# The whole ring of gathered rows filled one stage earlier, and the table of slots' experts made on partitions

## The chip, the cores and the metric

One core of one Trainium2 chip runs the whole program. The metric is the device time of one execution in microseconds (us). The kernel before takes 2877.39 us, the median of 3 runs (2876.5 to 2879.93).

## The reference, cut to what matters

A graph layer over 6250 nodes and 200000 edges (sorted by destination), then a mixture of 16 experts of which each node uses 2. Both add to the node's row.

```python
w_full = jnp.einsum('rb,bdo->rdo', w_comp, weight)          # R=16 relations from B=8 bases
x_rel = jnp.einsum('nd,rdo->rno', feat, w_full)             # feat = layernorm(x), 256 columns
msg = x_rel[etypes, src] * norm
agg = jax.ops.segment_sum(msg, dst, num_segments=N)
x = x + jax.nn.relu(agg + h_bias + feat @ loop_weight)
...
gate_logits = x @ gate_w + gate_b                           # x here: layernorm of the row
topk_vals, topk_idx = jax.lax.top_k(gate_logits, K)         # K=2 of E=16
topk_w = jax.nn.softmax(topk_vals, axis=-1)
h = jax.nn.relu(jnp.einsum('bsh,ehf->bsef', x, w1) + b1)
expert_out = jnp.einsum('bsef,efh->bseh', h, w2) + b2
...
y = x + moe
return (y - mu) / jnp.sqrt(var + EPS) * gamma + beta
```

## The kernel before, in words

The edges lie in 1568 blocks of 128. A step is one block against one window of 16 destination nodes; a block that crosses into a new window has a step for each, so that there are 1960 steps, seven to a turn. Destinations are dense at low node numbers, so the first window alone fills many blocks, and for these step number and block number are the same.

The stages follow one another as blocks of the program (`edges_in`, `sort_edges`, `steps`, `expand`, `graph_layer`, `route`, `experts`, `combine`). Between two stages all engines meet in a barrier: each engine drains, and none starts the next stage before the last has come. In the profile a barrier stands under the line of the stage that ends: L613 ends `expand` (its `with ctx:`), L891 ends `graph_layer`, L1467 ends `experts`.

**expand** (L607) makes the coefficients of the edges. GpSimd (POOL) fetches 16 groups of edge data by indirect DMA (L684), and between them gathers feature rows of the first blocks into the ring `rows` (L676): one indirect DMA per block, 128 rows of 256 floats. Before, 42 of the ring's 56 slots are filled here. TensorE (PE) and VectorE (DVE) make coefficients of the same groups; the later part goes to DRAM through SyncE's queue (L717), and SyncE waits at the end for these stores (L725).

```python
for q in range(EG + 1):                       # L672
    e.tensor_copy(idx[:, q * GB:(q + 1) * GB], srcT[:, q * GB:(q + 1) * GB]).then_inc(s_list, 1)
...
for j in range(3 * (SG - GR), EG * GB):       # L689
    ahead(j)
```

**graph_layer** (L885) goes through all steps. POOL gathers the remaining blocks in lists of GB = 14 (L978), each list into 14 slots of the ring; the list's indices are copied first (L960). For a list that goes into a slot used before, POOL waits until PE has done the steps of the blocks that lie there:

```python
for q in range(0 if later(i) else EG, IB):    # L965
    if later(i) or q >= RB // GB:
        e.wait_ge(s_P, free[q])               # L968
        e.sem_inc(s_turn, 1)
```

For the first such list, q = 4 (blocks 56 to 69, over blocks 0 to 13), `free[4]` is the first step of block 14, that is 14 steps. SyncE counts the gathered blocks on to PE (L941). PE first clears its accumulators with eight products of zeros (L1083, L1084), then for each turn loads a row of control words (L1166), branches over the code of a finished tile (L1168), waits for rows and coefficients, and issues seven steps, of two matmul records each (L1178). After every 16 windows it multiplies the tile by the bases (L1143). DVE builds the selection matrix of each turn (L1057) three turns ahead at most; for its turn n it waits until PE has done turn n - 4, except that turns 0 to 3 wait for nothing. So DVE's turn 5 starts when PE has done 14 steps. At the start of the stage SyncE and ScalarE also load the stage's weights and features (L934 to L937, L1191, L1195).

**route** (L1268) chooses the experts and sorts the pairs of node and expert into 114 slots of 128 rows. DVE makes the counts by prefix sums; `u` holds for each expert the number of the slot where it ends, the same on every partition. Then for 100 tiles DVE makes two one-hot operands (L1441, L1445) and PE sums their products (L1355). At the end DVE makes the table `slot_x` of the slots' experts (L1447 to L1450), clears `at_rows` (L1451), waits for PE and forms the rows' addresses (L1454 to L1459). Everything on DVE is one chain: each instruction waits for the one before.

Of the kernel before, what the change touches and what calls it, by code (L numbers as in the profile page):

```python
# [5 lines left out]
F32 = mybir.dt.float32  # L6
# [3 lines left out]
AX = mybir.AxisListType  # L10
P = 128
# [5 lines left out]
X, F, K = 16, 512, 2  # L17
# [61 lines left out]
RB = 56  # L79
GB = 14  # L80
QB = 7
IB = 2 * (RB // GB)
EG = RB // GB - 1
CTL_PART = (84, 72, 64, 60)
assert NBLK % RB == 0 and RB % GB == 0 and RB % QB == 0 and sum(CTL_PART) == TURNS and all(n % NS == 0 for n in CTL_PART)
assert all(t + n <= 8 * i <= TURNS for t, n, i in CHUNK)
# [2 lines left out]
SLOTS = (N * K + X * (P - 1)) // P  # L89
# [517 lines left out]
def expand(nc, d, w_comp, ident, tables, pairs, jcol, wcol, spread, dstS, wgtS, coefS, s_got, s_feat, srcT, idx, rows, s_row):  # L607
# [5 lines left out]
    with ctx:  # L613
# [53 lines left out]
        def _(e):  # L667
# [3 lines left out]
            e.iota(pno[:, :], [[0, 1]], base=-U, channel_multiplier=CN, allow_small_or_imprecise_dtypes=True).then_inc(s_const, 1)  # L671
            for q in range(EG + 1):  # L672
                e.tensor_copy(idx[:, q * GB:(q + 1) * GB], srcT[:, q * GB:(q + 1) * GB]).then_inc(s_list, 1)
# [211 lines left out]
def graph_layer(nc, d, a, ctl, pairs, room, wend, srcT, dstS, coefS, ident, wb, lw, hb, gw, s_w, logit, mean, rstd, idx, rows, s_row):  # L885
# [5 lines left out]
    with ctx:  # L891
# [96 lines left out]
        def _(e):  # L988
# [11 lines left out]

            def nodes(tile1, Q):

# [262 lines left out]
            e.wait_ge(s_st, 32 * (NT2 + 1))  # L1265


def route(nc, gate_b, w1, w2, logits, w1s, w2s, s_win, wgt, slot_x, at_rows):  # L1268


    from contextlib import ExitStack
    ctx = ExitStack()
    with ctx:
        def sb(name, shape, dt=F32):
            return ctx.enter_context(nc.sbuf_tensor(name, shape, dt))

        def sem(name):
            return ctx.enter_context(nc.semaphore(name))

        logit = sb("logit_b", [P, NT, X])  # L1280
# [10 lines left out]
        part = sb("part", [P, 1])  # L1291
# [5 lines left out]
        slots = sb("slots", [P, X])  # L1297
        end = [sb(f"end{k}", [P, X]) for k in range(2)]
        first = sb("first2", [P, X])
        slot_no = sb("slot_no", [1, SLOTS + 4])  # L1300
        ge = sb("ge", [1, SLOTS + 4, X])
        sx = sb("sx", [1, SLOTS + 4])
        pos = sb("pos", [P, NT, K], I32)
        part_i = sb("pos_part", [P, NT, K], I32)
        lo, hi, row = (sb(n, [P, NT, K]) for n in ("pos_lo", "pos_hi", "row_no"))
# [9 lines left out]
        psP = [ctx.enter_context(nc.psum_tensor(f"psP{k}", [P, 512], F32)) for k in range(2)]  # L1315
        psI = ctx.enter_context(nc.psum_tensor("psI", [P, 512], F32))
        s_w, s_c, s_d, s_df, s_e, s_b, s_p = (sem(n) for n in ("gate_b", "const", "dve", "diff", "exp", "both", "prefix"))
        s_lane, s_tile, s_inv = sem("lanes"), sem("tiles"), sem("inverse")
        Q = [(0, 25), (25, NT)]
        flat = "p t e -> p (t e)"  # L1320
        blk = ctx.enter_context(nc.Block())
# [11 lines left out]
        @blk.gpsimd  # L1333
        def _(e):
            e.iota(xno[:, :], [[1, X]], base=-X, channel_multiplier=0, allow_small_or_imprecise_dtypes=True).then_inc(s_c, 1)
            e.iota(lane[:, :], [[1, P]], base=0, channel_multiplier=0, allow_small_or_imprecise_dtypes=True).then_inc(s_c, 1)
            e.iota(part[:, :], [[0, 1]], base=0, channel_multiplier=1, allow_small_or_imprecise_dtypes=True).then_inc(s_c, 1)
            e.iota(slot_no[:, :], [[1, SLOTS + 4]], base=0, channel_multiplier=0, allow_small_or_imprecise_dtypes=True).then_inc(s_c, 1)
            e.iota(row[:, :, :].rearrange("p (t m) k -> p t (m k)", m=2), [[K * GN2, NT2], [1, 2 * K]], base=K, channel_multiplier=2 * K, allow_small_or_imprecise_dtypes=True).then_inc(s_c, 1)
            e.iota(tile_no[:, :], [[1, SLOTS]], base=0, channel_multiplier=0, allow_small_or_imprecise_dtypes=True).then_inc(s_c, 1)  # L1340
            e.iota(spare[:, :], [[P, SLOTS]], base=DUMP, channel_multiplier=1, allow_small_or_imprecise_dtypes=True).then_inc(s_c, 1)

        @blk.tensor
        def _(e):
            e.wait_ge(s_b, 1)
            for q, (t0, t1) in enumerate(Q):
                rhs = both[:, t0:t1, :].rearrange(flat)
                e.matmul(psP[q][:, 0:(t1 - t0) * X], tri[:, :], rhs, start=True, stop=True)
                last = e.matmul(psA[q][:, 0:(t1 - t0) * X], ones[:, :], rhs, start=True, stop=True)
            last.then_inc(s_p, 1)  # L1350
            for j in range(NT * K):
                if j % (GT * K) == 0:
                    e.wait_ge(s_lane, j // (GT * K) + 1)
                e.wait_ge(s_tile, j + 1)
                e.matmul(psI[:, 0:SLOTS], in_lane[j // (GT * K) % 2][:, j % (GT * K), :], in_tile[j % D][:, :], start=(j == 0), stop=(j == NT * K - 1)).then_inc(s_inv, 1)  # L1355
# [7 lines left out]
        def _(e):  # L1363
            ch = Chain(e, s_d)
# [4 lines left out]
            def over_e(a):  # L1369
                return a.unsqueeze(2).to_broadcast([P, NT, X])  # L1370

            e.wait_ge(s_c, 7)
            ch.add(e.memset(ones[:, :], 1.0))
            ch.add(e.tensor_scalar(tri[:, :], lane[:, :], part[:, 0:1], None, ALU.is_gt))
            ch.add(e.tensor_scalar(valid[:, :], part[:, :], float(TAIL), None, ALU.is_lt))
# [29 lines left out]
            a, b, sh = cum[0], cum[1], 1  # L1405
            while sh < NT:
                ch.add(e.tensor_copy(b[:, 0:sh, :], a[:, 0:sh, :]))
                ch(e.tensor_tensor(b[:, sh:NT, :], a[:, sh:NT, :], a[:, 0:NT - sh, :], ALU.add))
                a, b, sh = b, a, 2 * sh
# [5 lines left out]
            u, v, sh = end[0], end[1], 1  # L1415
            while sh < X:
                ch.add(e.tensor_copy(v[:, 0:sh], u[:, 0:sh]))
                ch(e.tensor_tensor(v[:, sh:X], u[:, sh:X], u[:, 0:X - sh], ALU.add))
                u, v, sh = v, u, 2 * sh
# [11 lines left out]
            ch(e.tensor_copy(lo[:, :, :], part_i[:, :, :]))  # L1431
            ch(e.tensor_single_scalar(part_i[:, :, :], pos[:, :, :], 7, ALU.arith_shift_right))
            ch(e.tensor_copy(hi[:, :, :], part_i[:, :, :]))

            for j in range(NT * K):
                t, k = divmod(j, K)
# [6 lines left out]
                if j >= D:  # L1443
                    e.wait_ge(s_inv, j - D + 1)
                e.tensor_scalar(in_tile[j % D][:, :], tile_no[:, :], hi[:, t, k:k + 1], row[:, t, k:k + 1], ALU.is_equal, ALU.mult).then_inc(s_tile, 1)  # L1445

            ch(e.tensor_tensor(ge[:, :, :], slot_no[:, :].unsqueeze(2).to_broadcast([1, SLOTS + 4, X]),  # L1447
                               u[0:1, :].unsqueeze(1).to_broadcast([1, SLOTS + 4, X]), ALU.is_ge))
            ch(e.tensor_reduce(sx[:, :], ge[:, :, :], AX.X, ALU.add))
            ch(e.tensor_scalar(slot_x[:, :], sx[:, :], float(X - 1), None, ALU.min))  # L1450
            ch(e.memset(at_rows[:, :, :], 0))  # L1451

            e.wait_ge(s_inv, NT * K)
# [392 lines left out]
def program(nc, a, out):  # L1846
    from contextlib import ExitStack
    ctx = ExitStack()
    d = Scratch(nc)

    with ctx:
        def sb(name, shape, dt=F32):
            return ctx.enter_context(nc.sbuf_tensor(name, shape, dt))

        def sems(name, n):
            return [ctx.enter_context(nc.semaphore(f"{name}{k}")) for k in range(n)]

        ident = sb("ident", [P, P])
        logit = sb("logit", [P, NT + 2, X])
        mean, rstd = sb("mean", [P, NT]), sb("rstd_h", [P, NT])  # L1860
        sent, got, s_row, s_xin, s_out, s_win = sems("sorted", 2), sems("got", 8), sems("row", RB // QB), sems("x_in", 2), sems("x_out", 2), sems("w_in", 4)
        with nc.sbuf_tensor("ident_i", [P, P], F32) as ident_i:
            identity(nc, ident, ident_i)
        gnn(nc, d, a, ident, sent, got, s_row, logit, mean, rstd)
        clear_semaphores(nc)
        wgt = sb("wgt", [P, NT, K])
        slot_x = sb("slot_x", [1, SLOTS + 4], I32)
        at_rows = sb("at_rows", [P, SLOTS + 4, 2], I32)
        with nc.sbuf_tensor("w1s", [P, X, HC, F], F32) as w1s, nc.sbuf_tensor("w2s", [P, X, FC, H], F32) as w2s:
            route(nc, a["L0_ffn_gate_b"], a["L0_ffn_w1"], a["L0_ffn_w2"], logit, w1s, w2s, s_win, wgt, slot_x, at_rows)  # L1870
            experts(nc, d, a["L0_ffn_b1"], a["L0_ffn_b2"], w1s, w2s, s_win, ident, slot_x, at_rows, s_xin, s_out)
        combine(nc, d, ident, mean, rstd, wgt, a["L0_ffn_gamma"], a["L0_ffn_beta"], out)

# [20 lines left out]
```

## Time and profile before

| | |
|---|---|
| median of 3 runs | 2877.39 us |
| the profiled execution | 2876.8 us |
| its span, first to last instruction | 2875.0 us |
| PE busy (matmul) | 2245.9 us, 78% |
| POOL busy | 1821.4 us, 63% |
| DVE busy | 964.7 us, 34% |
| `expand`, `graph_layer`, `route`, `experts` begin at about | 95, 180, 2191, 2276 us |

Busy time is what the engine's own instructions take; the time that POOL's sequencer needs between two indirect DMAs is not in it and stands as idle "issue". A row of a timeline gives the start, the duration, the engine and line, the operation with the tiles it writes and reads, and in brackets the idle time before it with what ended it. An engine name with a q is its sequencer: waits, branches, drains. All times are from the start of the span.

### The profile page before, as it was taken

To read this page: it belongs to the slowest core of one execution; us is meant where nothing else is said; L and a number is where in the kernel's file an instruction comes from. 1 tells how busy PE (TensorE), PEld (TensorE's weight loads), DVE (VectorE), ACT (ScalarE), POOL (GpSimd) and SP (SyncE) were. 2 spreads that over 40 slices of the span, in tenths; PEclk is the share of its full clock that TensorE was granted. 3 is DMA by queue.
4 is the path that set the end of the run, shared out by engine and by line. 5 is a ranking of instruction groups with operands and counts; after the bars stand their busy time and mean duration, and the time that the engine had idled before them with its cause. 6 is when DMAs were issued, how large, how long until landed. Compare 5 with 4: busy or idle time off the path is not lost. (4 is left out here: it accounts for less than half of the span.)

```text
span 2875.0 us, 41253 instructions
## 1 busy us (share of the span) xinstructions
PE 2245.9 (78%) x11563; PEld 1848.7 (64%) x11564; DVE 964.7 (34%) x2255; ACT 591.0 (21%) x1382; POOL 1821.4 (63%) x2003
## 2 busy tenths in 40 slices
PE   1676566766776787888888998999993699999977
PEld 0455444644665666676676776878782588888765
DVE  6762111121212221222232232242425733333338
ACT  2100000101011111122222222232330022222245
POOL 0467777777777777777777777777710144554444
PEclk9787777887888898999999999999996899999998
DMA  6363333343334434444444444444425211111246
GB/s 234 91 192 104 104 105 105 104 122 115 108 116 122 119 118 116 118 134 120 119 121 131 130 123 127 122 126 127 129 49 189 100 63 64 62 63 61 62 156 241
DMA packets 146352, 338.78 MB, mean 118 GB/s; under 512 B 36707, under 2 KB 56323, under 8 KB 146148
## 3 DMA queue, kind: packets, MB, share of 16 engines
q0 software_dynamic: 89392, 245.59, 29.4%
q1 hardware_dynamic: 39311, 59.54, 6.0%
q10 hardware_dynamic: 17588, 32.88, 3.4%
q8 instruction: 34, 0.56, 0.1%
q14 instruction: 27, 0.21, 0.0%
HBM read 293.10 MB, written 47.97 MB: 119 GB/s over the span
## 5 line engine op out<-in xcount | busy, mean ns | idle before, releaser
L978 POOL DMA_INDIRECT rows<-feat,idx x1526 | 1447.9, 949 | 450.0 <-issue 436.3
L1178 PE MATMUL psW<-rows,S 128*128 x3920 | 1062.6, 434 | 358.0 <-SPq L941 325.4
L1178 PEld LDWEIGHTS psW<-rows,S 128*128 128x128 f32 x3920 | 843.0, 219 | 573.0 <-issue 435.3
L1057 DVE TENSOR_TENSOR S<-psHere,coefS 128x896 f32<-128x896 f32 x280 | 303.2, 1091 | 1385.9 <-PE psW L1178 1379.8
L1236 ACT COPY z<-psW 128x512 f32<-128x512 f32 x196 | 114.9, 586 | 1363.1 <-PE psW L1178 1360.6
L1143 PE MATMUL psG<-wb,zT 128*128 128x256 f32 (+1 forms) x1600 | 353.5, 379 | 0.0
L1143 PEld LDWEIGHTS psG<-wb,zT 128*128 128x128 f32 (+1 forms) x1600 | 300.6, 188 | 44.7
L1509 POOL DMA_INDIRECT xs<-y_rows,at x114 | 116.3, 1020 | 211.3 <-DVE os L1624 211.0
L1565 PE MATMUL psH<-xT,w1x 128*128 128x128 f32 x1840 | 228.0, 277 | 0.3 <-DVE w1x L1607 0.3
L1538 ACT ACTIVATE hT<-psH,b1T 128x128 f32<-128x128 f32 x460 | 131.5, 368 | 428.1 <-PE psH L1565 428.1
L1565 PEld LDWEIGHTS psH<-xT,w1x 128*128 128x128 f32 x1840 | 215.9, 193 | 1.3 <-issue 0.6
L1574 PE MATMUL psO<-w2s,hT 128*128 x912 | 215.7, 379 | 0.0
L1574 PEld LDWEIGHTS psO<-w2s,hT 128*128 128x128 f32 x912 | 164.6, 190 | 17.6
L1522 POOL DMA_INDIRECT expert_rows<-os,at x114 | 120.5, 1057 | 38.5 <-issue 36.3
L1624 DVE TENSOR_TENSOR os<-psO,b_b 128x256 f32<-128x256 f32 x114 | 48.4, 425 | 238.2 <-PE psO L1574 238.2
L1130 PE MATMUL psZ<-ident,z 128*128 128x128 f32 x784 | 113.7, 283 | 13.6 <-ACT zT L1250 8.9
L1238 ACT COPY psW<-zero 128x512 f32<-128x512 f32 x196 | 115.5, 589 | 6.2
L1250 ACT COPY zT<-psZ 128x512 f32<-128x512 f32 x196 | 108.0, 589 | 18.6 <-PE psZ L1130 18.6
L1130 PEld LDWEIGHTS psZ<-ident,z 128*128 128x128 f32 x784 | 83.7, 141 | 36.2 <-ACT zT L1250 20.3
L1555 PE MATMUL psX<-ident,xs 128*128 128x128 f32 x232 | 49.4, 295 | 43.4 <-DMA xs<-y_rows,at 37.6
L1607 DVE COPY w1x<-w1s 128x1024 f32 x116 | 80.0, 690 | 0.2 <-issue 0.2
L1555 PEld LDWEIGHTS psX<-ident,xs 128*128 128x128 f32 x232 | 25.3, 142 | 78.5 <-issue 54.6
(256 smaller groups left out, 1429.8 us busy)
## 6 DMA issues: line engine op xcount, KB each, us to landing
rows<-feat,idx POOLq DMA_INDIRECT x1568
g<-expert_rows SPq DMA_DIRECT2D x24, 512.0 KB, 6.1
w1s<-in_L_ffn_w SPq DMA_DIRECT2D x8, 1024.0 KB, 10.9
w2s<-in_L_ffn_w SPq DMA_DIRECT2D x16, 512.0 KB, 10.9
feat<-rows SPq DMA_DIRECT2D x24, 256.0 KB, 4.4
fts<-feat ACTq DMA_DIRECT2D x24, 256.0 KB
h<-in_x ACTq DMA_DIRECT2D x24, 256.0 KB
y_rows<-y ACTq DMA_DIRECT2D x24, 256.0 KB
```

Of the source, the lines that this page charges most:

```text
L978: e.indirect_dma_start(rows[:, at * H:(at + 1) * H], None, d.feat, bass.IndirectOffsetOnAxis(ap=idx[:, q * GB + u:q * GB + u + 1], axis=0) ...
L1057: e.tensor_tensor(S[h0 + h][:, :].rearrange("p (s b n) -> p s b n", s=U, b=B), both[:, h * U:(h + 1) * U, :].unsqueeze(2).to_broadcast([P, ...
L1130: last = e.transpose(to[:, k * P:(k + 1) * P], z[:, w * H + c * P:w * H + (c + 1) * P], ident[:, :])
L1143: last = e.matmul(psG[0:Q, m * H:(m + 1) * H], zT[:, at:at + Q], wb[:, c, b, :], start=False, stop=(c == HC - 1 and b == B - 1))
L1178: e.matmul(psW[:, bass.ds(bank[u], H)], S[h][:, u * ZC:(u + 1) * ZC], rows[:, bass.ds(slot[u], H)], start=False, stop=True, skip_group_che ...
L1236: e.copy(z[:, 2 * k * H:2 * (k + 1) * H], bank).then_inc(s_z, 1)
L1238: e.copy(bank.rearrange("p (w o) -> p w o", w=2), zero[:, :].unsqueeze(1).to_broadcast([P, 2, H])).then_inc(s_clear, 1)
L1509: e.indirect_dma_start(xs[k][:, :], None, d.y, bass.IndirectOffsetOnAxis(ap=column, axis=0)).then_inc(s_in[k], 16)
L1522: e.indirect_dma_start(d.two, bass.IndirectOffsetOnAxis(ap=at[k][:, 1:2], axis=0), os_[k][:, :], None).then_inc(s_out[k], 16)
L1538: last = e.activation(hT[k][:, c * P:(c + 1) * P], psH[k][:, c * P:(c + 1) * P], ACT.Relu, bias=b1T[:, bass.ds(ex * FC + c, 1)])
L1565: last = e.matmul(psH[k][:, f * P:(f + 1) * P], w1x[k][:, c * F + f * P:c * F + (f + 1) * P], xT[k][:, c * P:(c + 1) * P], start=(c == 0), ...
L1574: last = e.matmul(psO[k][:, 0:H], hT[k][:, c * P:(c + 1) * P], w2s[:, bass.ds(ex, 1), c, :].rearrange("p e f -> p (e f)"), start=(c == 0), ...
```

## The change

Two edits that have nothing to do with one another.

The first is one constant: EG, the number of lists of 14 gathered in `expand`, goes from 3 to 4. All 56 slots of the ring are gathered there; five lists of indices are copied instead of four; and `graph_layer` starts its loop at q = 4, the first list that waits.

The second is in `route`. Slot numbers no longer lie along one partition but across partitions: each partition p compares the 16 ends with its own number, sums and clips (three small instructions, before the 100 tiles). PE turns this column into a row with the identity matrix, ahead of the tiles' products, and DVE copies the row out of PSUM to `slot_x` after the tiles. The iota of slot numbers goes.

```diff
-EG = RB // GB - 1
+EG = RB // GB
...
-def route(nc, gate_b, w1, w2, logits, w1s, w2s, s_win, wgt, slot_x, at_rows):
+def route(nc, ident, gate_b, w1, w2, logits, w1s, w2s, s_win, wgt, slot_x, at_rows):
...
-        slot_no = sb("slot_no", [1, SLOTS + 4])
-        ge = sb("ge", [1, SLOTS + 4, X])
-        sx = sb("sx", [1, SLOTS + 4])
+        ge = sb("ge", [P, X])
+        sx = sb("sx", [P, 1])
...
+        psX = ctx.enter_context(nc.psum_tensor("psSlot", [P, 512], F32))
...
+        s_sx, s_sxt = sem("slot_experts"), sem("slot_experts_row")
...
-            e.iota(slot_no[:, :], [[1, SLOTS + 4]], base=0, channel_multiplier=0, allow_small_or_imprecise_dtypes=True).then_inc(s_c, 1)
...
             last.then_inc(s_p, 1)
+            e.wait_ge(s_sx, 1)
+            e.matmul(psX[0:1, 0:P], sx[:, 0:1], ident[:, :], start=True, stop=True).then_inc(s_sxt, 1)
             for j in range(NT * K):
...
-            e.wait_ge(s_c, 7)
+            e.wait_ge(s_c, 6)
...
             ch(e.tensor_copy(hi[:, :, :], part_i[:, :, :]))
+            ch(e.tensor_scalar(ge[:, :], u[:, :], part[:, 0:1], None, ALU.is_le))
+            ch(e.tensor_reduce(sx[:, :], ge[:, :], AX.X, ALU.add))
+            ch(e.tensor_scalar(sx[:, :], sx[:, :], float(X - 1), None, ALU.min))
+            e.sem_inc(s_sx, 1)
...
-            ch(e.tensor_tensor(ge[:, :, :], slot_no[:, :].unsqueeze(2).to_broadcast([1, SLOTS + 4, X]),
-                               u[0:1, :].unsqueeze(1).to_broadcast([1, SLOTS + 4, X]), ALU.is_ge))
-            ch(e.tensor_reduce(sx[:, :], ge[:, :, :], AX.X, ALU.add))
-            ch(e.tensor_scalar(slot_x[:, :], sx[:, :], float(X - 1), None, ALU.min))
+            e.wait_ge(s_sxt, 1)
+            ch(e.tensor_copy(slot_x[:, :], psX[0:1, 0:SLOTS + 4]))
             ch(e.memset(at_rows[:, :, :], 0))
```

What this does to the order on POOL, from the last group of edge data in `expand` (L684) over its end (L613) into `graph_layer` (from L953); L676 and L978 are gathers of blocks, L960 the copy of a list's indices:

```order
 L684 DMA edge<-edge_blocks,jcol 128x384
-L676 DMA rows<-feat,idx 128x256 x21
+L676 DMA rows<-feat,idx 128x256 x35
 L613 UNCONDITIONAL_BRANCH
 L953 UNCONDITIONAL_BRANCH
@@ -59,6 +59,4 @@
 L963 TENSOR_LOAD tables
 L964 ISA
-L960 COPY idx<-srcT 128x14
-L978 DMA rows<-feat,idx 128x256 x14
 L960 COPY idx<-srcT 128x14
 L978 DMA rows<-feat,idx 128x256 x14
```

Fourteen gathers moved from behind the barrier L613 to before it. What is now the first list behind the barrier is the one that waits for 14 steps.

On DVE in `route`, before the change, the end of the prefix sums, the tiles (ten groups, the last shown), and what follows them up to the product's result `psI`:

```order
L1433 CAST pos_hi<-pos_part 128x100
L1441 TENSOR_TENSOR in_lane<-lane,pos_lo 128x1280
L1445 TENSOR_SCALAR in_tile<-tile_no,pos_hi,row_no 128x114 x10
L1447 TENSOR_TENSOR ge<-slot_no,end 1x1888
L1449 TENSOR_REDUCE sx<-ge 1x118
L1450 TENSOR_SCALAR slot_x<-sx 1x118
L1451 MEMSET at_rows 128x236
L1454 COPY found<-psI 128x114
```

The same places after the change, where lines are numbered 2 to 6 higher:

```order
L1435 CAST pos_hi<-pos_part 128x100
L1436 TENSOR_SCALAR ge<-end,part 128x16
L1437 TENSOR_REDUCE sx<-ge 128x1
L1438 TENSOR_SCALAR sx<-sx 128x1
L1447 TENSOR_TENSOR in_lane<-lane,pos_lo 128x1280
L1451 TENSOR_SCALAR in_tile<-tile_no,pos_hi,row_no 128x114 x10
L1454 CAST slot_x<-psSlot 1x118
L1455 MEMSET at_rows 128x236
L1458 COPY found<-psI 128x114
```

Two instructions of 1888 elements on one partition and a small one have gone from behind the tiles; three small ones stand before the tiles, and one copy behind them.

## Rows read from the trace of the kernel before

**Rows 1.** Page, its head and its group of gathers.
```profile
span 2875.0 us, 41253 instructions
...
L978 POOL DMA_INDIRECT rows<-feat,idx x1526 | 1447.9, 949 | 450.0 <-issue 436.3
```

**Rows 2.** Waits of POOL: engine line, releaser, us in total, times, longest.
```profile
POOL rows L978 <- PE psW L1178: 13.7, 45, 0.3
```

**Rows 3.** Timeline of PE, late waits for rows: start, duration us.
```profile
1780.66 9.66 PE L1178 MATMUL psW<-rows,S 128*128 x36 [5.12 <-SPq L941]
...
2078.15 3.28 PE L1178 MATMUL psW<-rows,S 128*128 x14 [0.26 <-SPq L941]
```

**Rows 4.** Timeline of POOL about the end of expand.
```profile
170.51 0.95 POOL L676 DMA_INDIRECT rows<-feat,idx  x1 [0.30 <-issue]
...
181.69 0.99 POOL L978 DMA_INDIRECT rows<-feat,idx  x1 [0.49 <-issue]
...
198.01 0.94 POOL L978 DMA_INDIRECT rows<-feat,idx  x1 [0.30 <-issue]
...
199.47 0.97 POOL L978 DMA_INDIRECT rows<-feat,idx  x1 [0.31 <-issue]
```

**Rows 5.** Timeline of SyncE's queue over the same barrier.
```profile
160.72 17.37 SPq L717 DMA_DIRECT2D late_coefs<-late  x15
179.99 1.02 SPq L934 DMA_DIRECT2D wb<-in_L_gnn_weight  x2
```

**Rows 6.** POOL's drains, by line: duration ns min/median/max, first and last start us.
```profile
L613 POOLq DRAIN  x1: 21683/21683/21683, 156.5 to 156.5; - x1
...
L891 POOLq DRAIN  x1: 21631/21631/21631, 2087.5 to 2087.5; - x1
...
L1467 POOLq DRAIN  x1: 1049/1049/1049, 2776.1 to 2776.1; - x1
```

**Rows 7.** Timelines of POOL before drains L891 and L1467, of SyncE's queue after the latter.
```profile
2101.53 0.95 POOL L978 DMA_INDIRECT rows<-feat,idx  x1 [0.30 <-issue]
...
2772.81 0.99 POOL L1522 DMA_INDIRECT expert_rows<-os,at  x1 [0.30 <-issue]
...
2777.36 0.34 SPq L1673 DMA_DIRECT2D hi<-h_rows  x1
```

**Rows 8.** Timelines of PE and DVE, the first 14 steps.
```profile
186.96 4.26 PE L1178 MATMUL psW<-rows,S 128*128 x19
194.62 4.00 PE L1178 MATMUL psW<-rows,S 128*128 x9 [3.40 <-issue]
...
198.81 1.09 DVE L1057 TENSOR_TENSOR S<-psHere,coefS 128x896 f32<-128x896 f32 x1 [7.42 <-PE psW L1178]
```

**Rows 9.** Windows: engines' busy us, then PE clock, DMA share, GB/s.
```profile
188.00:190.00 2.00, 2.00 (x11) 1.74 (x11) 0.00 (x0) 0.00 (x0) 1.70 (x2) 1.00 1.09 348
...
194.60:198.70 4.10, 4.00 (x9) 2.58 (x8) 0.00 (x0) 0.00 (x0) 3.19 (x4) 0.50 0.40 114
```

**Rows 10.** PE's branch L1168 in 196:200.5, ns min/median/max, start.
```profile
L1168 PEldq COMPARE_BRANCH  x1: 3281/3281/3281, 196.8 to 196.8; - x1
```

**Rows 11.** Timeline of DVE in route: start, two small steps, after the tiles.
```profile
2193.95 0.99 DVE L1377 TENSOR_TENSOR logit_b<-logit,gb 128x800 f32<-128x800 f32 x1 [0.94 <-DMA gb<-in_L_ffn_gate_b]
...
2220.40 0.17 DVE L1420 TENSOR_TENSOR first<-end,slots 128x16 f32<-128x16 f32 x1
2220.61 0.17 DVE L1421 TENSOR_SCALAR first<-first 128x16 f32<-128x16 f32 x1
...
2268.68 2.11 DVE L1447 TENSOR_TENSOR ge<-slot_no,end 1x1888 f32<-1x1888 f32 x1
...
2273.29 0.26 DVE L1451 MEMSET at_rows<- 128x236 int32 x1
2273.58 0.28 DVE L1454 COPY found<-psI 128x114 f32<-128x114 f32 x1
```

**Rows 12.** Timeline of PE in route, its last group of products.
```profile
2266.67 2.62 PE L1355 MATMUL psI<-in_tile,in_lane 128*128 128x114 f32 x20 [1.26 <-DVE in_tile L1445]
```

More of the change, by code:

```diff
@@ L1869, in program @@
         with nc.sbuf_tensor("w1s", [P, X, HC, F], F32) as w1s, nc.sbuf_tensor("w2s", [P, X, FC, H], F32) as w2s:
-            route(nc, a["L0_ffn_gate_b"], a["L0_ffn_w1"], a["L0_ffn_w2"], logit, w1s, w2s, s_win, wgt, slot_x, at_rows)
+            route(nc, ident, a["L0_ffn_gate_b"], a["L0_ffn_w1"], a["L0_ffn_w2"], logit, w1s, w2s, s_win, wgt, slot_x, at_rows)
             experts(nc, d, a["L0_ffn_b1"], a["L0_ffn_b2"], w1s, w2s, s_win, ident, slot_x, at_rows, s_xin, s_out)
```

## The prediction, written before the changed kernel ran

> **What bounds the kernel now.** I read the page first. GpSimd issues 1526 gathers in `graph_layer`, 0.949 us busy each, with 436.3 us of idle "issue" between them [rows 1]: (1447.9 + 436.3) / 1526 gives 1.23 us for each, and 1526 of them, with the lists' copies between, fill some 1920 us of the 2875 us span. The waits of POOL come next: on TensorE it waited 13.7 us in all, 0.3 us at the longest [rows 2]. So POOL never stands still in this stage: it is one stream from its first gather to its last, and the ring's limit of 56 blocks never holds it. Then the timeline of TensorE, for where the stream sets the end: at 1780.66 PE had waited 5.12 us for rows, at 2078.15 another 0.26 us [rows 3]. The first is far from the end, but behind it PE is nearly always busy, and the second shows that the stream is again just behind PE near the end. So a stream that runs D later moves PE's wait at 1780, all that follows it, and the end, by D. A stream that runs earlier would move the earlier waits, and so this one, in the same way.
>
> The question of the first edit is therefore only when block 56 is gathered. In the timeline of POOL about the barrier [rows 4] the last of the 42 gathers ends at 170.51 + 0.95 = 171.46; the first of `graph_layer` starts at 181.69; fourteen of them, 1.255 us apart ((198.01 - 181.69) / 13), end at 198.95; block 56 starts at 199.47. SyncE opens the stage at 179.99; call this T. Its stores of coefficients have gone out until 178.09 [rows 5].
>
> **The first edit, step by step.** What it removes behind the barrier is 14 gathers, 17.5 us of POOL. They were free there: block 56 goes over block 0, so its list waits for 14 steps, and PE has done these just before DVE's turn 5 at 198.81 [rows 8], some 0.1 us earlier: 198.7, T + 18.7. The gathers end 0.25 us after that. I take 0.8 us from PE's 14th step to block 56 (199.47 - 198.7), for list copy and dispatch.
>
> What it adds before the barrier is the same 17.5 us. `expand` has no such room: the last gather ends at 171.46 + 17.5 = 188.95, and the others are done by 180 [rows 5]. One more copy of a list stands before the edge groups, where POOL later waits for them anyway; I count 0 (at most 0.2 us, by the copy's size).
>
> Then the barrier itself. POOL's drain at L613 starts at 156.5, since the sequencer is ahead of its engine, and lasts 21.68 us, to 178.2 [rows 6]: 6.7 us longer than the last gather. At the end of `graph_layer` the drain lasts from 2087.5 to 2109.1, the last gather ends at 2102.48 [rows 6, 7]: again 6.7 us, though nothing else was the same. At the end of `experts` it ends at 2777.1, only 3.3 us after the last indirect DMA at 2773.80; there POOL had waited for its transfers before the drain, and SyncE opens the next stage 0.2 us behind it [rows 6, 7]. The case here is that of the first two. So in the profile before, the drain ended 1.8 us ahead of T and cost nothing; that cover is gone: 188.95 + 6.7 + 0.2 = 195.9 is the new T, 15.9 us later. Between 3.3 and 6.7 us for the drain I take 6.7; the lower end gives 12.5 us.
>
> The Trainium skill, "PSUM — Partial Sum Buffer", section "Engine vs sequencer instructions", says that a drain waits until the engine is fully idle. By that alone it would end with the gather row, T would be 189.2 and not 195.9, and the sum below 6.7 us smaller. The trace has an idle POOL engine and a drain that goes on, twice; I keep this as a rival.
>
> How long do PE's first 14 steps take behind the new T? Before, 18.7 us. The products of zeros and the first 19 records of steps are the same. Then PE stands still from about 191.2 to 194.62, in the middle of a turn, for nothing that is named, and its clock, at full speed (1.00, 2.4 GHz) in 188 to 190 with the DMA engines full at 348 GB/s, is at 0.50 (1.2 GHz) from 194.6 on, where 9 records take 4.00 us, 0.44 apart [rows 8, 9]. I read the pause as a fetch of instructions, since the same happens two turns on: the branch L1168 takes 3.28 us at 196.8, with the DMA engines at 0.40 [rows 9, 10]. At the first place the DMA engines carried the stage's weights and POOL's gathers together. In the changed kernel the gathers are gone from there; the pause may shorten by about 1.4 us (an estimate: what the crowded fetch, about 4.7 us from the last issued step, has over the quiet 3.28 us). If the clock then stays up, 4.5 steps take 0.43 us each (by the 19 records in 4.26 us, about 0.22 us a record) instead of 0.86: 1.9 us more. I take half of that: 2.3 us less, T + 16.4. The bounds are 1 us more (a worse phase of the clock) and 5.6 us less (no pause at all).
>
> The Trainium skill speaks against this gain: "DMA: Bandwidth & Descriptors", section "Queues, rings and completion order", says that each DMA engine serves its rows in turn, a packet at a time. By that a fetch on its own row loses hardly anything to gathers, the 2.3 us would be 0, and the sum 2889.7. The two pauses here, of different length, lean the other way, but no run here has them apart.
>
> So block 56 starts at 195.9 + 16.4 + 0.8 = 213.1 instead of 199.47: D = 13.6 us later. Nothing gives this back: later lists wait at most 0.3 us before [rows 2], and 14 gathers take 17.6 us where PE at full clock needs some 6 for 14 steps.
>
> **The second edit.** Behind the tiles, from the start of `ge` at 2268.68 to `found` at 2273.58 DVE needs 4.90 us [rows 11]. Now there are a copy out of PSUM (0.28 us as the copy of `psI`, 0.04 between) and the memset (0.26), 0.62 us in all; but PE's last product ends at 2266.67 + 2.62 = 2269.29 [rows 12], so that `found` can't start before about 2269.35, 0.7 us after 2268.68. That removes 4.2 us. Ahead of the tiles stand three small operations more, 0.21 us from start to start [rows 11], 0.6 us, and everything behind moves with them, PE's products too. PE's extra product waits for the third of them and has the 1.5 us of DVE's first `in_lane` to run in: 0, at most 0.3 us. The iota of POOL: 0, since DVE's first work ends a wait of 0.94 us for `gate_b` [rows 11]. The sum is -3.6 us, with bounds -3.2 and -3.9. `route` ends with DVE, so all of it counts.
>
> **Sum.** Profiled execution 2876.8 us; +13.6 and -3.6 give 2886.8. The median of the runs lies 0.6 us above the profiled one: 2887.4 us.
>
> **The rivals.**
> - *The drain costs nothing beyond the last gather.* Then T is 189.2, D = 6.9 us, and with -3.6 the time is 2880.7 us; with the pause gone as well (5.6 instead of 2.3 us) 2877.4. That is no change, and the case on the other side: the whole verdict hangs on the 6.7 us behind POOL's last gather. Against it stand both drains [rows 6, 7].
> - *The gathers find cover*, as if `expand` had room for them and the next list could start at once: 17.5 us off the stream, capped by nothing before 1780, and -3.6: 2856 us. For it is only that the ring would be full earlier. Against it: SyncE is done at 180, POOL's last gather would end at 189, and the list behind it waits for steps that PE can't begin before the barrier.
> - *The table's new way loses its gain*: DVE meets PE's turned row late, or the tiles start in another phase of PE's clock; the 3.6 us are 0 and the time is 2891.0 us. Against it: 1.5 us of cover, and PE's order puts the product first.
>
> **Chances.** The forecast (drain of 3.3 to 6.7 us, pause between its bounds) 0.83; the first rival 0.08, the second 0.03, the third 0.06. The range of 8 in 10 takes in the drain's lower part and the pause's bounds: the drain at 5 us with 2.3 us more from PE would be 2883.4, the third rival 2891.0; I take 2882.5 to 2891. A measurement of this kernel tells a change of over 0.2%, 5.8 us, from none. Slower by more than that (above 2883.2) is the forecast but for its lowest part, and the third rival: 0.86. Within: the first rival and that lowest part, 0.11. Faster: 0.03.
>
> **What would show it.** In the new profile POOL's last gather of `expand` ends near 189, its drain near 195.7, and SyncE's first load of weights starts near 195.9. POOL's first gather of `graph_layer` comes near 213, some 24 us behind the end of the last one of `expand`; the last of all ends near 2116. DVE's turn 5 tells PE's 14th step: near T + 16.5. In `route` the two instructions of 2.11 us are gone, and `found` starts some 0.7 us after the last of the tiles' operands has gone out, where it was 4.9 us. A T near 189 would prove the drain wrong, a first gather right behind T the wait; a stream that is 13 us late while the end is not would prove wrong that POOL's stream sets the end.

## The result, and the profile after

Eight runs of each on the same chip: the kernel before 2877.25 us median (2874.94 to 2879.93), the changed kernel 2886.15 us (2884.91 to 2888.05). The ratio is 1.0031, 95% interval 1.0020 to 1.0042: 8.9 us slower. Its profiled execution took 2887.5 us. The head of its page and the group of gathers behind the barrier answer to [rows 1]; 14 gathers have left the group:

```profile
span 2885.7 us, 41270 instructions
...
L978 POOL DMA_INDIRECT rows<-feat,idx x1512 | 1435.1, 949 | 445.7 <-issue 430.8
```

The timeline of POOL about the end of `expand`, and its last gather of `graph_layer` (start, duration, operation, idle time before and what ended it), for [rows 4, 7]:

```profile
188.29 0.94 POOL L676 DMA_INDIRECT rows<-feat,idx  x1 [0.30 <-issue]
195.46 0.16 POOL L979 IOTA z<- 128x16 f32 x1 [6.23 <-POOLq L613]
210.43 0.20 POOL L960 COPY idx<-srcT 128x14 int32<-128x14 int32 x1 [14.80 <-PE psW L1178]
211.12 0.99 POOL L978 DMA_INDIRECT rows<-feat,idx  x1 [0.49 <-issue]
...
2112.69 0.94 POOL L978 DMA_INDIRECT rows<-feat,idx  x1 [0.30 <-issue]
```

The last gather ahead of the barrier ends at 189.23, where it was 171.46. POOL then waits 6.23 us for its own drain, and 14.8 us behind the barrier for PE's 14 steps. Block 56 comes at 211.12 instead of 199.47, 11.65 us later, and the last gather of all at 2112.69 instead of 2101.53, 11.16 us later. SyncE's queue, for [rows 5], and POOL's drain, for [rows 6] (duration in ns three times, start):

```profile
151.15 27.08 SPq L717 DMA_DIRECT2D late_coefs<-late  x25
195.45 1.02 SPq L934 DMA_DIRECT2D wb<-in_L_gnn_weight  x2
```

```profile
L613 POOLq DRAIN  x1: 20928/20928/20928, 174.3 to 174.3; - x1
```

Before, SyncE's stores had gone out at 178.09 and the stage opened at 179.99; here they are out at the same time (178.23), and the stage waits for POOL until 195.45. The drain ends at 174.3 + 20.93 = 195.2, 5.96 us behind the last gather. Timelines of PE and DVE behind the barrier, for [rows 8]:

```profile
200.94 3.18 PE L1178 MATMUL psW<-rows,S 128*128 x14
205.01 1.34 PE L1178 MATMUL psW<-rows,S 128*128 x5 [0.88 <-issue]
208.14 2.12 PE L1178 MATMUL psW<-rows,S 128*128 x9 [1.79 <-issue]
```

```profile
210.45 1.09 DVE L1057 TENSOR_TENSOR S<-psHere,coefS 128x896 f32<-128x896 f32 x1 [5.07 <-PE psW L1178]
```

DVE's turn 5 comes 15.0 us behind the first load; it was 18.8. PE's late waits for rows, for [rows 3], are the same two, 10.05 and 11.15 us later, and POOL's wait for PE, for [rows 2], is as small as it was:

```profile
1790.71 5.86 PE L1178 MATMUL psW<-rows,S 128*128 x13 [4.89 <-SPq L941]
...
2089.30 3.28 PE L1178 MATMUL psW<-rows,S 128*128 x14 [0.26 <-SPq L941]
```

```profile
POOL rows L978 <- PE psW L1178: 14.9, 49, 0.3
```

The timelines of DVE and PE in `route`, for [rows 11, 12]:

```profile
2239.71 0.23 DVE L1436 TENSOR_SCALAR ge<-end,part 128x16 f32<-128x16 f32 x1
2239.98 0.17 DVE L1437 TENSOR_REDUCE sx<-ge 128x1 f32<-128x16 f32 x1
2240.18 0.15 DVE L1438 TENSOR_SCALAR sx<-sx 128x1 f32<-128x1 f32 x1
2240.50 1.49 DVE L1447 TENSOR_TENSOR in_lane<-lane,pos_lo 128x1280 f32<-128x1280 f32 x1 [0.16 <-DVE sx L1438]
...
2280.60 0.26 DVE L1454 CAST slot_x<-psSlot 1x118 int32<-1x118 f32 x1
2280.98 0.26 DVE L1455 MEMSET at_rows<- 128x236 int32 x1
2281.32 0.28 DVE L1458 COPY found<-psI 128x114 f32<-128x114 f32 x1
```

```profile
2278.58 2.63 PE L1357 MATMUL psI<-in_tile,in_lane 128*128 128x114 f32 x20 [1.26 <-DVE in_tile L1451]
```

The two instructions of 2.11 us are gone; three small ones stand ahead of the tiles, 0.79 us from `ge` to `in_lane`; `found` starts 0.72 us behind `slot_x`. From SyncE's load of `gb` to its load of `b_rows` the stage takes 81.01 us (2202.46 to 2283.47), where it took 84.43 (2191.30 to 2275.73): 3.42 us less. `experts` and `combine` read 1.0 and 2.0 us longer in this one execution; how they vary is told with the first edit alone.

### The profile page after: what moved, and what is told of

Read it like the earlier page. It is cut to its first block and busy times, and to the rows that moved or that the text cites. A ratio compares the mean times of both kernels' runs of the same rounds, so it can differ in the third digit from the quotient of the medians.

```text
span 2885.7 us, 41270 instructions
## 1 busy us (share of the span) xinstructions
PE 2230.9 (77%) x11565; PEld 1837.3 (64%) x11566; DVE 959.0 (33%) x2256; ACT 590.4 (20%) x1382; POOL 1823.2 (63%) x2002
## 5 line engine op out<-in xcount | busy, mean ns | idle before, releaser
L978 POOL DMA_INDIRECT rows<-feat,idx x1512 | 1435.1, 949 | 445.7 <-issue 430.8
L1178 PE MATMUL psW<-rows,S 128*128 x3920 | 1044.9, 428 | 373.3 <-SPq L941 335.8
L1178 PEld LDWEIGHTS psW<-rows,S 128*128 128x128 f32 x3920 | 831.2, 216 | 582.2 <-issue 449.0
L1130 PE MATMUL psZ<-ident,z 128*128 128x128 f32 x784 | 113.7, 283 | 13.6 <-ACT zT L1250 8.9
L1607 DVE COPY xT<-psX 128x256 f32<-128x256 f32 x116 | 48.9, 421 | 84.4 <-PE psX L1559 45.2
```

The source lines that it names most:

```text
L978: e.indirect_dma_start(rows[:, at * H:(at + 1) * H], None, d.feat, bass.IndirectOffsetOnAxis(ap=idx[:, q * GB + u:q * GB + u + 1], axis=0) ...
L1130: last = e.transpose(to[:, k * P:(k + 1) * P], z[:, w * H + c * P:w * H + (c + 1) * P], ident[:, :])
L1178: e.matmul(psW[:, bass.ds(bank[u], H)], S[h][:, u * ZC:(u + 1) * ZC], rows[:, bass.ds(slot[u], H)], start=False, stop=True, skip_group_che ...
```

## The experiments

All runs are ratios against the kernel before on the same chip. One thing must be known first. In the comparison above and on the chips of f1, f6 and f7 (called good here) the kernel before took 2877 to 2882 us; on three others (called slow; the first five runs, and f2 to f5) it took 3754 to 3766. What those show is told at the end. Their stage behind the barrier is another regime, in which POOL waits 687 us for PE (f3); but where POOL issues no gathers, their traces run like the others, and so the drain and the first 14 steps can be read from them.

**The first edit alone** (before, with `EG` changed), three times.

```
-EG = RB // GB - 1
+EG = RB // GB
```

> The first edit alone: 56 blocks ahead, the table the old way. My theory: SyncE's first weights load at 195.5 us (last gather 189.2 plus POOL's drain), block 56 at 211.1, POOL's last gather of graph_layer near 2113.6, the route stage 84.4 us; the time is about 11.3 us above the kernel before, 2888.6 us, with 1 to 2 us more if the later stages were really longer. Rival (the new table costs time behind route, so that part of the 8.9 us is its doing): under 9 us above.

> The first edit alone once more (56 blocks ahead, the table the old way), for a chip on which the kernel before takes about 2877 us. My theory: first weights load at 195.5 us, block 56 at 211.1, POOL's last gather of graph_layer near 2113.6, route 84.4 us; 11.3 us above the kernel before. Rival (part of the changed kernel's 8.9 us comes from the new table, behind route): under 9 us above. On a chip on which the kernel before takes over 3700 us: first weights load near 249, since the other engines hardly move beside the gathers, and some 15 to 30 us above before.

> The first edit alone, a third time, for a chip on which the kernel before takes about 2877 to 2882 us. My theory (the edits add up): last gather of expand at 189.2, POOL's drain 5.96 us behind it, first weights load at 195.5 us, block 56 at 211.1, POOL's last gather of graph_layer near 2113.6, route 84.4 us; 11 to 12.5 us above the kernel before, since the changed kernel was 8.9 above with a route 3.4 us shorter. Rival (part of the changed kernel's 8.9 us comes from the new table, behind route): 9 us above or less. On a chip on which the kernel before takes over 3700 us: the first load near 243 to 249 and the time within 0.8% of before.

The third fell on a chip where the kernel before takes 2877.51 us: 2890.29 us, ratio 1.0047 (1.0033 to 1.0060), 12.8 us slower. Its timeline of POOL:

```profile
188.36 0.94 POOL L676 DMA_INDIRECT rows<-feat,idx  x1 [0.30 <-issue]
195.53 0.16 POOL L979 IOTA z<- 128x16 f32 x1 [6.23 <-POOLq L613]
...
211.16 0.99 POOL L978 DMA_INDIRECT rows<-feat,idx  x1 [0.49 <-issue]
...
2114.20 0.95 POOL L978 DMA_INDIRECT rows<-feat,idx  x1 [0.30 <-issue]
```

It repeats the changed kernel's times within 0.1 us up to block 56; its last gather comes 1.5 us later than there. The ring costs 12.8 us (by the interval 9.5 to 17), more than the 9 of the rival, and the changed kernel 8.9. The difference of 3.9 fits the 3.4 of the stage, but the two intervals together are wider than it, so what the table does is read by stages. In the seven profiles with the old table `route` takes 84.3 to 85.7 us (84.46 here), in the seven with the new one 80.98 to 81.12. `combine` is the same with either (97.2 to 99.3, 97.4 to 99.6). `experts` takes 501.3 to 502.2 us with the old table and 501.8 to 504.5 with the new one, medians 501.7 and 502.0: a cost of some tenths behind `route` stays open. On the slow chips the same kernel gave 1.0078 (1.0049 to 1.0107) and 0.9975 (0.9942 to 1.0008): there chips differ by more than the intervals say, and I take no verdict from their times.

**The second edit alone** (the changed kernel with `EG` as before), twice, both on slow chips.

```
-EG = RB // GB
+EG = RB // GB - 1
```

> The second edit alone: 42 blocks ahead of the barrier as before, the table of slots' experts made the new way. My theory (the two edits act in different stages and add up): SyncE's first weights load stays near 180.0 us and POOL's last gather of graph_layer near 2102.5, as before; route takes 81.0 us instead of 84.4, and the time is 3.4 us below the kernel before, about 2873.8 us. Rival (the table's gain is taken back later, or is the run's scatter): the route stage is shorter but the time is that of before, 2877.2 us.

> The second edit alone once more (42 blocks ahead, the new table), for a chip on which the kernel before takes about 2877 us. My theory (the edits act in different stages and add up): first weights load near 180.0 us, POOL's last gather of graph_layer near 2102.5, route 81.0 us instead of 84.4; 3.4 us below the kernel before. Rival (the table's gain is taken back behind route): route is shorter, the time is that of before. On a chip on which the kernel before takes over 3700 us: route 81.1 us, the rest within its scatter.

Ratios 1.0007 (0.9984 to 1.0030) and 1.0006 (0.9972 to 1.0040): 3.4 us can't be seen there. The stage can: `route` takes 81.06 and 81.01 us.

**The ring the other way**: 28 blocks ahead.

```
-EG = RB // GB - 1
+EG = RB // GB - 2
...
-                    for j in range(3 * (g - GR), 3 * (g - GR + 1)):
+                    for j in range(3 * (g - GR), min(EG * GB, 3 * (g - GR + 1))):
```

> The edit the other way round, on the kernel before: only 28 blocks ahead of the barrier and 28 behind it, table the old way. My theory (POOL's stream behind the barrier sets the end, and only 14 of its gathers have cover beside PE's first 14 steps): SyncE's first weights load stays at 180.0, since POOL's drain was not what ended last there; the 28 gathers behind it need 14 x 1.255 + 0.4 = 17.9 us more, block 56 starts near 217.4, and the time is 17.9 us above before, about 2895 us. Rival (the ring is full enough, and what costs time in the changed kernel is only its longer expand): the time is that of before, 2877 us, or less.

> The kernel of e3 once more (28 blocks ahead of the barrier, 28 behind it, table the old way). The first five runs fell on chips on which the kernel before itself takes 3754 to 3766 us instead of 2877: there PE, DVE and the semaphores between engines hardly moved while POOL issued gathers, and fewer gathers ahead made it 13 us faster. On a chip on which the kernel before takes 2877 us, where the other engines work beside the gathers: my theory says first weights load near 180, block 56 near 217.4, 17.9 us slower than before, about 2895 us; the rival (the longer expand alone costs time) says no slower than before. If this chip is again a slow one: POOL's last gather of expand near 173, first weights load near 210, and 10 to 15 us below the kernel before.

On the good chip 2896.26 us against 2881.67, ratio 1.0050 (1.0033 to 1.0067), 14.6 us slower. The timeline of POOL at its block 56, and its last gather:

```profile
179.47 0.16 POOL L979 IOTA z<- 128x16 f32 x1 [25.00 <-POOLq L613]
...
216.08 0.21 POOL L960 COPY idx<-srcT 128x14 int32<-128x14 int32 x1
216.45 0.97 POOL L978 DMA_INDIRECT rows<-feat,idx  x1 [0.16 <-issue]
...
2121.53 0.95 POOL L978 DMA_INDIRECT rows<-feat,idx  x1 [0.30 <-issue]
```

The stage opens when it did (0.5 us earlier) and the stream is 17.0 us late at block 56. At the last gather it is 20.0 us later than in the trace of before: on this chip, where before takes 4 us more, a gather took 951 ns on the mean instead of 949, some 3 us over 1540 of them. So both directions lose: fewer gathers ahead leave uncovered ones behind the barrier, more leave uncovered ones ahead of it. It refutes the rival that only the longer `expand` costs. The time is 3.3 us under the 17.9 expected, inside its interval. On the slow chip the sign was the other one, 0.9964 (0.9941 to 0.9987), for the reason below.

**Half of it**: 49 blocks ahead, 7 behind; on a slow chip.

```
-            for j in range(3 * (SG - GR), EG * GB):
+            for j in range(3 * (SG - GR), 49):
...
-                    for u in range(GB):
+                    for u in range(49 - EG * GB if not later(i) and q == EG else 0, GB):
```

> The first edit by half, on the kernel before: 49 blocks ahead, the last 7 of the ring behind the barrier, table the old way. My theory (the end of expand is the last gather plus POOL's drain of 6.0 to 6.7 us plus 0.2): last gather at 171.46 + 7 x 1.25 = 180.2, SyncE's first weights load at 186.4 to 187.1, 6.4 to 7.1 us late; 7 gathers behind the barrier are hidden beside PE's first 14 steps, so block 56 comes 15.8 to 19.5 us behind, and the time is 3.5 to 7 us above before, about 2882.5 us. Rival (a drain that costs nothing beyond the last gather): first weights load at 180.4, the time that of before. Second rival (a step: all 56 ahead is what costs, a part is free): the time that of before or below.

1.0039 (1.0015 to 1.0064), but not by my mechanism: the stage opened at 239.20, where SyncE's stores ended last, and so the law "last gather plus drain" was not tried. What it gives is the drain. Where SyncE's stores had not begun or were over (DMA share 0.08 to 0.14 during those us), the drain ended 3.67 us behind the last gather for 28 blocks ahead, 4.82 for 42, 5.39 for 49, 5.96 for 56. Here are POOL's rows of L613 for 42 and 49; the last gathers end at 186.19 and 199.58:

```profile
L613 POOLq DRAIN  x1: 19798/19798/19798, 171.2 to 171.2; - x1
```

```profile
L613 POOLq DRAIN  x1: 20410/20410/20410, 184.6 to 184.6; - x1
```

That is 0.082 us for each gather more. Counted with the 16 indirect DMAs of edge data in the same block, it is 0.083 us for each of 44 to 72 (an estimate from these four), with next to nothing besides. Where SyncE's stores run beside it (DMA share 0.48 to 0.59), it is longer: 4.6 for 28 on the good chip, 6.2 for 43 (f6), 6.7 for 42 in the kernel before. PE and DVE work there too, so that the stores are the cause is argued, not shown.

**A wait before the drain**, added to the changed kernel; both on slow chips.

```
             for j in range(3 * (SG - GR), EG * GB):
                 ahead(j)
+            for q in range(RB // QB):
+                e.wait_ge(s_row[q], 16 * QB)
```

> The changed kernel (56 blocks ahead, new table) with one thing more: at the end of expand POOL waits until all its 56 gathers have landed, and only then drains. In the changed kernel the drain ended 5.96 us behind the last gather. My theory (the drain waits for what the gathers still have under way, whatever the sequencer waits for first): the transfers' landing is a part of these 6 us that is waited for anyway, the drain behind it is short, and SyncE's first weights load stands where it stood, 6 to 6.5 us behind POOL's last gather, within 1 us; the time is that of the changed kernel, near 2886 us where the kernel before takes 2877. Rival (the drain has a length of its own, of some 3 us or more, that begins when the sequencer gets there, as at the end of experts: 3.3 us behind the last DMA): landing and drain add up, the first load comes 2 to 4 us later than in the changed kernel. Second rival (the drain works off something that POOL's idle sequencer does faster): it comes earlier.

> The changed kernel with POOL waiting at the end of expand until its 56 gathers have landed, before it drains; once more, for a chip on which the kernel before takes about 2877 us. My theory (the drain waits for what the gathers still have under way, whatever the sequencer waits for first): first weights load 6 to 6.5 us behind POOL's last gather, as in the changed kernel (195.5), within 1 us, and the time of the changed kernel, 8.9 us above before. Rival (the drain has a length of its own that begins when the sequencer gets there): landing and drain add up, the first load 2 to 4 us later; on the slow chip the drain ended 8.0 us behind the last gather, which leans to this one. Second rival (the drain works off something that an idle sequencer does faster): earlier.

```profile
L613 POOLq DRAIN  x1: 5950/5950/5950, 206.0 to 206.0; - x1
```

My theory fell. POOL's sequencer saw the last row landed 2.1 us behind the last gather (203.89 to 205.98), and only then the drain began, and took the same 5.95 us; it ended 8.04 us behind the gather, in the other run 8.03. In the changed kernel itself no DMA packet moves from 191.5 us on, and the drain lasts to 195.2. So the drain is no wait for transfers: it has a length of its own, and 56 landed gathers cost as much as 56 under way. The times (0.9978 and 0.9999, intervals over 1) say nothing, since the drain is off the path on these chips.

**The weights later**, in the changed kernel; on a slow chip.

```
+            rows_in(0)
+            e.wait_ge(s_P, 14)
             (the six loads of wb, lw, hb, gw)
-            i0 = 0
+            i0 = 1
```

> The changed kernel with SyncE's six loads of the stage's weights moved behind PE's 14th step; PE needs them first for a tile's product, hundreds of steps on. POOL has no gather there before block 56, so the DMA engines are idle during the first 14 steps but for fetches of instructions. My theory (the pause in PE's turn is a fetch that the crowded DMA engines lengthen: 4.7 us with weights and gathers in the kernel before, 2.9 us with weights alone in the changed one): the pause shortens again, by up to 1.5 us, DVE's turn 5 comes at T + 13.5 to 14.5 instead of T + 15.0, and block 56 and the end as much earlier; on the time 0 to 1.5 us below the changed kernel, 7.5 to 9 us above before. Rival (a fetch takes its time whatever else moves, and what shortened the first 14 steps in the changed kernel was only the clock): turn 5 stays at T + 15.0 within 0.3 us, unless the clock steps elsewhere. Second rival (POOL's first gathers now meet the weights): block 56 and its followers come late, and the time is above the changed kernel.

The timelines of DVE and PE (its own line numbers):

```profile
256.24 1.09 DVE L1059 TENSOR_TENSOR S<-psHere,coefS 128x896 f32<-128x896 f32 x1 [2.73 <-PE psW L1180]
```

```profile
249.09 4.26 PE L1180 MATMUL psW<-rows,S 128*128 x19
253.93 2.12 PE L1180 MATMUL psW<-rows,S 128*128 x9 [0.58 <-issue]
```

The stage opened at 242.75; turn 5 comes 13.5 us behind it, where the two runs of the ring alone on such chips had 14.9 and 15.2 with pauses of about 2 us. The pause is 0.58 us, and the transfer of instructions that ends it starts 8.2 us behind the opening, in f3 on the same chip 10.2 us. The weights put it off. The time, 1.0025 (0.9990 to 1.0060), doesn't tell.

**What the runs point to**: the new table, 43 blocks ahead (as above, with 43 for 49), the weights later.

> What the runs so far point to: the new table; 43 blocks ahead of the barrier (one more than before, since POOL's drain had 1.8 us of room before SyncE's first load), 13 behind it; and SyncE's loads of the weights behind PE's 14th step. My theory, on a chip on which the kernel before takes about 2877 us: POOL's last gather of expand ends near 172.7, its drain near 179.5, graph_layer starts at 180.0 to 180.2 as before; the 13 gathers end 1.25 us earlier than the 14 did, and PE's 14th step, freed of the weights' crowding, comes by about 1.5 us earlier (18.8 to 17.3 us behind the start), so block 56 starts near 198.3 instead of 199.47; with route 3.4 us shorter the time is 4.5 us below the kernel before and 13 us below the changed one. Rival (the weights now meet POOL's gathers behind block 56, which costs the 1.1 us or more): 3.4 us below the kernel before or less. On a chip on which the kernel before takes over 3700 us: graph_layer starts 1 to 2 us later than with 42 ahead, and the time is that of before within its scatter.

2876.22 us against 2882.01 on that chip, ratio 0.9982 (0.9973 to 0.9991): 5.8 us by the medians, 5.2 by the ratio, where 4.5 was expected (interval 2.6 to 7.8). By the ratios it beats both kernels.

```profile
172.18 0.95 POOL L676 DMA_INDIRECT rows<-feat,idx  x1 [0.30 <-issue]
180.87 0.16 POOL L981 IOTA z<- 128x16 f32 x1 [7.75 <-POOLq L613]
...
198.59 0.20 POOL L962 COPY idx<-srcT 128x14 int32<-128x14 int32 x1
198.96 0.97 POOL L980 DMA_INDIRECT rows<-feat,idx  x1 [0.16 <-issue]
...
2102.17 0.95 POOL L980 DMA_INDIRECT rows<-feat,idx  x1 [0.30 <-issue]
```

```profile
186.35 4.26 PE L1180 MATMUL psW<-rows,S 128*128 x19
190.77 2.12 PE L1180 MATMUL psW<-rows,S 128*128 x9 [0.16 <-issue]
```

`route` takes 80.98 us. The stage opens 0.9 us late, because PE's and SyncE's own work in `expand` ended that much later, and POOL's stream is then the bound with no idle time, since PE's 14th step comes 12.2 us behind the opening. Block 56 is 0.5 us earlier than before, not 1.1, and the last gather is 0.64 us later than in the trace of before, taken on another chip. The weights go out at 200.49, 7.6 us behind the 14th step, since SyncE first waits there for all 56 blocks. So the traces show the table's gain of 3.4 us, and none of the 43 blocks and the later weights that reaches the end; how the time divides was not run apart on a good chip.

## Why the prediction was right, step by step

- *Last gather of `expand` at 188.95*: 189.23. The 14 gathers had no room there.
- *Drain 6.7 us*: 5.96, in all five profiles with 56 ahead that have no wait added. The verdict hung on it, and it held: with a free drain the stage would have opened at 189.4. But I had taken 6.7 for one fixed length. It grows with the gathers, and the 6.7 of before was 4.8 for 42 gathers and 1.9 more beside the stores. The second witness was chance: the drain at the end of `graph_layer`, 6.7 us behind the last gather before, is 9.2 us behind it in the changed kernel. The agreement was partly luck. T was 195.45, for 195.9.
- *First 14 steps T + 16.4*: T + 15.0. This is the term that was mis-sized: -3.8 us instead of -2.3. By the rows of PE, the last 9 records start 12.7 us behind T instead of 14.6 (1.9 less, for 1.4), and they take 2.12 us at full clock instead of 4.00 at half (1.9 less; I had taken half of this). The first step also comes earlier, 5.5 us behind T instead of 7.0, because the clock rises earlier during the products of zeros (granted 0.68 over 195.5 to 200.9, 0.53 before over 180 to 186.9). That gave nothing: the first 19 records, with a new pause of 0.88 us, take 1.2 us more, and the second pause ends with a fetch. In e1 the first step comes at T + 6.1 and the 9 records still start at T + 14.5. The bound of 5.6 us less for no pause at all adds up to 5.4 by its own terms.
- *Why the pause shortens*: I said, because the gathers are gone. The transfers of instructions bear this out. Queue q8 carries them, 16 KB each; one falls into 191.9 to 193.2 before and one into 205.5 to 206.7 after (packets, MB, share of the DMA engines):

```profile
q8 instruction: 1, 0.02, 5.1%
```

```profile
q8 instruction: 1, 0.02, 5.8%
```

They start at T + 12.0 and T + 10.1, and PE goes on 2.6 us later in both. The same transfer starts at T + 11.8 to 12.1 in all six profiles with weights and gathers behind the barrier, at T + 10.1 to 10.6 in all six with weights alone, at T + 8.2 with neither (f5) and at T + 7.6 with gathers alone (f6). Each takes 0.9 to 1.4 us, and PE goes on 2.3 to 3.0 us behind its start. So the gathers put the fetch off by 1.3 us or more beside the weights, and by nothing that the two runs without them show; the weights put it off by 1.9 us or more. The rule of the Trainium skill that I held against the gain ("DMA: Bandwidth & Descriptors", section "Queues, rings and completion order": each DMA engine serves its rows in turn, a packet at a time) had given me a gain of 0. It was 3.8 us, and the measurements decide.
- *A drain ends when the engine is idle* ("PSUM — Partial Sum Buffer", section "Engine vs sequencer instructions", the Trainium skill): for POOL behind indirect DMAs that is not the whole of it: the drain took 5.95 us with no POOL instruction running in the trace and every row landed.
- *D = 13.6 us and nothing gives it back*: D was 11.65 at block 56 and 11.15 at the last gather. PE's two late waits for rows moved with it. The mechanism, one stream of POOL that sets the end, holds in both directions (f1, f7); over the 1900 us from block 56 to the last gather the four other traces from good chips differ from before's by -0.5 to +3.0 us.
- *The second edit -3.6 us*: -3.42. 0.8 us ahead of the tiles for 0.6; the rest as worked out.
- *Sum*: +11.15 - 3.42 = +7.7 us, and +8.9 measured. The 1.2 us between are within the runs' interval of 5.8 to 12.1 us. In the two profiled executions the difference is 10.7 us, with the 3.0 of `experts` and `combine`, which I had at nothing. So that 2887.4 came so near 2886.15 is in part luck: D was 2 us too large, and the later stages made up for some of it.

## What to carry to other kernels

Work moved ahead of a barrier is only cheaper if the engine that does it isn't the one that then ends last: compare its end, its drain included, with the end of every other engine there, and count what it was hidden behind on the other side. Here 28 and 56 ahead both lost against 42; 43 was run only together with two other edits. Loads of data that is needed late (weights) can keep an engine from its instructions at the start of a stage: without them PE's fetch came 1.9 us or more earlier. No run shows apart what issuing them later is worth in time.

## What the runs showed of the hardware that I had not expected

POOL's drain ends 3.67 us behind the last of 28 gathers (and 16 other indirect DMAs of the block) and 0.082 us later for each further one up to 56; with 56 it takes 5.95 us even when every row has landed. Why, no run here shows. At the end of `graph_layer` it is 6.7 us behind 1526 gathers before and 9.2 us behind 1512 in the changed kernel, so that it doesn't go on growing so, and what sets it there is open.

On three chips the same kernel takes 31% longer (3766 us for 2877). `route`, `experts` and `combine` take the same there (e1: 81.06, 502.45 and 97.68 us). What differs, in the windows read, is the stretches in which POOL issues gathers back to back: the gathers keep their 0.95 us, and the other engines nearly stop. The windows of the kernel before on a good chip, and of e1 on a slow one (busy us and instructions of PE, weight load, DVE, ACT, POOL):

```profile
165.00:190.00 25.00, 16.93 (x179) 13.66 (x175) 17.12 (x34) 0.96 (x5) 11.78 (x15) 0.80 0.71 221
```

```profile
165.00:190.00 25.00, 4.78 (x59) 3.75 (x56) 2.76 (x5) 0.00 (x0) 18.90 (x21) 0.57 0.36 107
200.00:225.00 25.00, 19.73 (x399) 15.56 (x397) 24.87 (x53) 3.48 (x17) 0.00 (x0) 0.99 0.35 119
```

DVE does 5 instructions in the 25 us in which POOL gathers, and 53 in 25 us once it has stopped. PE's sequencer shows where: its step of arithmetic at L1176 never takes over 36 ns on the good chip, and up to 715 ns here (in 300:900 us, of before and of e1):

```profile
L1176 PEldq ALU_OP  x76: 32/36/36, 306.6 to 896.8; - x76
```

```profile
L1176 PEldq ALU_OP  x59: 3/36/715, 302.3 to 863.1; - x59
```

So on such a chip a gather ahead of the barrier has no cover at all: with 28, 42, 49 and 56 ahead the stage opens at 210.4, 230.0, 239.2 and 248.7 us, 1.3 to 1.4 us a gather. What these chips have in common, and whether it is contention for the sequencers' access or for semaphores, stays open.
